# A two-layer attention and expert network on one core: softmax denominators by block transposes with additions a head at a time, query and key projections as half-column pairs, and another order of steps among the experts

## What is computed

```python
def layer(x, attention, network):
    xn = layernorm(x)
    return x + attention(xn) * silu(network(xn))

# first layer: attention over the 16 heads of each token; network of 16 experts, two chosen per token:
routed = combine[:, 15:16] * flat
for e in range(15):
    y = (silu(flat @ gate_w[e]) * (flat @ up_w[e])) @ down_w[e]
    routed = routed + combine[:, e:e+1] * y      # and a shared expert with a convolution in its gate

# second layer: attention over the 1024 tokens of a sequence, 16 heads of 64
xr = xn / norm(xn) * sqrt(128) * (gamma + 1)
q, k, v = split(xr @ w_qkv)
sim = (q * 64 ** -0.5) @ k.T
out = softmax(sim, axis=-1) @ v                  # the denominator is the sum of exp over the keys
s = out.reshape(b, n, 1024) @ w_out
# network: three layers of 512 with weights of -1, 0 and 1 and a scale each
```

## Time and profile before

| | |
|---|---|
| median of 3 runs | 1085.93 us (1085.88 to 1086.94) |
| profiled execution | 1085.6 us, span 1083.8 us |
| PE busy | 1065.5 us (98%) |
| DVE, POOL, ACT busy | 799.9, 794.4, 577.2 us |
| granted clock of PE, mean | 0.999 |

### The profile page before, as it was taken

One profiled execution on the slowest core, in us unless ns is written; L12 is line 12 of the kernel. 1 busy time (PEld: TensorE's weight loads), 2 busy tenths in 40 slices (PEclk: granted clock), 3 DMA queues, 4 the chain that ended last, 5 costly groups with the idle time before them and its releaser, 6 DMA issues.

```text
span 1083.8 us, 21982 instructions
## 1 busy us (share of the span) xinstructions
PE 1065.5 (98%) x8715; PEld 675.5 (62%) x8715; DVE 799.9 (74%) x1249; ACT 577.2 (53%) x923; POOL 794.4 (73%) x515
## 2 busy tenths in 40 slices
PE   9999999899999999999999999999999999999998
PEld 7898898777655455455455555555555455467886
DVE  4658866587776878877887887887888877895553
ACT  4634453565555555555555555555555555654442
POOL 5778997645567898898898899899899898940000
PEclk9999999999999999999999999999999999999999
DMA  7323234533100000200000000000000000000000
GB/s 234 134 80 100 101 117 127 159 112 107 35 1 1 1 1 2 108 1 1 1 1 1 1 2 1 1 2 1 1 2 2 1 1 2 1 1 10 11 1 20
DMA packets 32678, 40.22 MB, mean 37 GB/s; under 512 B 4544, under 2 KB 24384, under 8 KB 31296
## 3 DMA queue, kind: packets, MB, share of 16 engines
q1 hardware_dynamic: 32256, 38.80, 10.9%
q10 hardware_dynamic: 320, 0.01, 0.0%
HBM read 28.97 MB, written 9.70 MB: 36 GB/s over the span
## 4 chain that ended last, share of the span: by engine, by line
PE 74%; DVE 3%; ACT 1%; issue 1%; SPq 0%; DMA 0%; DVEq 0%; ACTq 0%
PE o_ps L1735 21%; PE mx_ps L1688 7%; PE st_ps L1707 5%; PE st_ps L1713 5%; PE st_ps L1710 5%; PE bank L2142 3%; PE bank L2143 3%; PE bank L2144 3%; PE mx_ps L1626 3%; PE pj_ps L1640 3%; PE pj_ps L1632 2%; PE mx_ps L1620 2%; PE st_ps L1719 1%; PE mx_ps L1622 1%; PE mx_ps L1621 1%; DVE mx_part L1947 1%
## 5 line engine op out<-in xcount | busy, mean ns | idle before, releaser
L2054 POOL TENSOR_TENSOR acc<-acc,prob 128x1024 f32<-128x1024 f32 x192 | 468.7, 2441 | 47.3 <-ACT prob L1881 37.1
L1881 ACT ACTIVATE prob<-st_ps 128x1024 f32<-128x1024 f32 x256 | 248.6, 1023 | 197.7 <-PE st_ps L1719 103.6
L1735 PE MATMUL o_ps<-prob,v_cur 128*64 128x512 f32 x1024 | 246.4, 602 | 0.0
L1944 DVE TENSOR_REDUCE mx_part<-mx_ps 128x1 f32<-128x512 f32 x258 | 164.7, 666 | 58.3 <-PE mx_ps L1688 58.3
L1947 DVE TENSOR_REDUCE mx_part<-mx_ps 128x2 f32<-128x1024 f32 x78 | 93.5, 1199 | 60.8 <-PE mx_ps L1688 60.8
L1735 PEld LDWEIGHTS o_ps<-prob,v_cur 128*64 128x64 f32 x1024 | 63.8, 136 | 108.9 <-issue 72.7
L1969 DVE RECIPROCAL rden<-rden 128x128 f32<-128x128 f32 x128 | 119.5, 934 | 0.0
L1688 PEld LDWEIGHTS mx_ps<-k_hi,q_hi 64*128 64x128 f32 x414 | 46.5, 183 | 107.4 <-issue 72.6
L1688 PE MATMUL mx_ps<-k_hi,q_hi 64*128 64x512 f32 x414 | 111.8, 457 | 1.4 <-DVE mx_part L1947 0.6
L2054 POOL TENSOR_TENSOR acc<-prob 128x1024 f32<-128x1024 f32 x32 | 76.6, 2393 | 34.1 <-ACT prob L1881 33.0
L1713 PE MATMUL st_ps<-q_hi,d_lo 64*128 64x512 f32 x512 | 100.9, 390 | 0.0
(11 more groups left out here) (404 smaller groups left out, 2209.7 us busy)
## 6 DMA issues: line engine op xcount, KB each, us to landing
w_tile<-w_rows SPq DMA_DIRECT2D x72, 128.0 KB, 2.9
v_rows<-ha_v SPq DMA_DIRECT2D x8, 1024.0 KB, 4.2
ha_vt<-v_rows SPq DMA_DIRECT2D x16, 512.0 KB, 4.1
q_max<-mx_turned SPq DMA_DIRECT2D x128, 1.0 KB
h_w<-in_h SPq DMA_DIRECT2D x2, 1024.0 KB, 7.9
w_raw<-in_w SPq DMA_DIRECT2D x8, 192.0 KB, 3.7
head_wkv<-in_wkv SPq DMA_DIRECT2D x2, 512.0 KB, 4.8
m_w<-in_m SPq DMA_DIRECT2D x3, 256.0 KB, 3.0
```

Of the source, the lines that this page charges most:

```text
L1735: mm = pe.matmul(o_ps[rows(h), :], v_cur[:, m % 2, j, rows(h)], prob[:, (16 * m + slot) % RING, h, :], start=(j == 0), stop=(j == KT - 1), ...
L1881: act.activation(prob[:, n % RING, :, :], st_ps[:, slot % 2, :, :], ACT.Exp, scale=SCALE).then_inc(s_exp, 1)
L1944: dve.reduce_max(mx_part[:, h, i, keys:keys + 1], maxima_banks(q, n)[h], AX_X).then_inc(s_mxr, 1)
L2054: pool.tensor_tensor(total, old, new, ALU.add).then_inc(s_acc, 1)
```

## The change

It has five parts.

- **Denominators.** POOL adds a head at a time, 28 additions of 512 columns instead of 14 of 1024. DVE turns `acc` of a half (1024 columns) in blocks of 32 x 32 (`turned`) and sums each run of 32, so that `den_part` holds one sum a token for 32 partitions. PE adds the four blocks of partitions by `lanes`, with 16 columns a head instead of 512. ACT copies 16 columns, DVE inverts them, and a second block transpose of their repetition spreads them out into `rden`. `INVERT` goes; `DEN_TURN`, `DEN_SUM`, `DEN_BACK` and `NORMALIZE` say in which batch each step stands. The `den` unit of half 1 moves from batch 1 to batch 2 on PE.
- **Queries and keys.** A `qk` unit is two plain `F32` products of 64 columns of weights each, for the two heads, instead of three `F32R` ones of 128. The splits of `w_raw` and of `xr` go, on ACT, DVE and POOL.
- **Experts.** On ACT, `gate` and `sq` stand ahead of the Silu of the iteration.
- **Handover.** `e.scalar_x` is a turn earlier on ACT; on PE the gates of iteration 3 and the down product of iteration 0 stand between the last turns of the first attention.
- **End of the attention.** The low parts of the last network's weights `h2` are made on POOL behind its additions, no longer on DVE; x's split for chunk 0 moves from DVE to ACT and POOL; the last units stand in other places (`AFTER_END`).

```diff
-    FIRST = ("sq",)
+    FIRST = ("gate", "sq")
...
     def scalar(act, n):
         k, e = n // EPAIRS, n % EPAIRS
-        if n < ALL:
-            act.wait_ge(s_g, n + 1)
-            act.activation(g_ps[n % 2], g_ps[n % 2], ACT.Silu).then_inc(s_sg, 1)
         kn, names = norms(n)
         for name in names:
             if name in FIRST:
                 scalar_norm(act, kn, name)
+        if n < ALL:
+            act.wait_ge(s_g, n + 1)
+            act.activation(g_ps[n % 2], g_ps[n % 2], ACT.Silu).then_inc(s_sg, 1)
...
+    DEN_TURN, DEN_SUM, DEN_BACK = {1: (1, -1), 4: (0, 0)}, {2: (1, -1), 5: (0, 0)}, {3: (1, -1), 6: (0, 0)}
+    NORMALIZE = {5: (1, -1), 7: (0, 0)}
...
-    AFTER = {1: ("den", 1), 3: ("out", 0), 5: ("den", 0), 7: ("out", 1)}
+    AFTER = {2: ("den", 1), 3: ("out", 0), 5: ("den", 0), 7: ("out", 1)}
+    AFTER_END = {1: ("out", 0), 2: ("den", 1), 7: ("out", 1)}
...
-            hi, lo = xr_hi[:, chunk(q, half), :], xr_lo[:, chunk(q, half), :]
-            pe.matmul(to, w_hi[:, p, tile(t)], hi, start=True, stop=False)
-            pe.matmul(to, w_hi[:, p, tile(t)], lo, start=False, stop=False)
-            mm = pe.matmul(to, w_lo[:, p, tile(t)], hi, start=False, stop=True)
+            for h in range(2):
+                of = slice(t * P + h * HD, t * P + h * HD + HD)
+                mm = pe.matmul(to[rows(h), :], w_raw[:, p, of], xr[:, chunk(q, half), :], start=True, stop=True,
+                               skip_group_check=True)
...
-            pe.wait_ge(s_acc, ADDS * q + 7 * (half + 1))
+            pe.wait_ge(s_turns, den_done(q, u[1], "summed"))
             for h in range(2):
-                mm = pe.matmul(pj_ps[rows(h), :], c.ones[:, 0:HD], acc[:, half, h, :],
+                mm = pe.matmul(pj_ps[rows(h), 0:DEN], lanes[:, :], den_part[:, h * DEN:h * DEN + DEN],
                                start=True, stop=True, skip_group_check=True)
...
-            act.activation(rden[:, half, :], pj_ps[:, :], ACT.Copy).then_inc(s_den, 1)
+            act.activation(den_out[:, :], pj_ps[:, 0:DEN], ACT.Copy).then_inc(s_den, 1)
...
-        dve.reciprocal(part, part).then_inc(s_rcp, 1)
+    def vector_den_turn(dve, q, half):
...
+        dve.wait_ge(s_acc, 2 * (ADDS * q + 7 * (half + 1)))
+        dve.transpose(turned[:, :], acc[:, half, :, :].rearrange("p h n -> p (h n)")).then_inc(s_turns, 1)
+
+    def vector_den_sum(dve, q, half):
+        dve.wait_ge(s_turns, den_done(q, half, "turned"))
...
+        dve.reduce_sum(den_part[:, :], turned[:, :].rearrange("p (n r) -> p n r", r=LANES), AX_X).then_inc(s_turns, 1)
+
+    def vector_den_back(dve, q, half):
+        dve.wait_ge(s_den, 2 * q + half + 1)
...
+        dve.reciprocal(den_rcp[:, :], den_out[:, :]).then_inc(s_turns, 1)
+        dve.wait_ge(s_turns, den_done(q, half, "inverse"))
+        dve.transpose(rden[:, half, :].rearrange("p (n r) -> p n r", r=LANES),
+                      den_rcp[:, :].unsqueeze(2).to_broadcast([P, DEN, LANES])).then_inc(s_turns, 1)
...
-        pool.tensor_tensor(total, old, new, ALU.add).then_inc(s_acc, 1)
+        for h in range(2):
+            new, total = prob[:, (16 * m + slot) % RING, h, :], acc[:, half, h, :]
+            old = prob[:, (16 * m + slot - 1) % RING, h, :] if j == 1 else total
+            if j > 1:
+                pool.wait_ge(s_acc, 2 * (ADDS * m + 7 * half + j - 2) + h + 1)
+            pool.tensor_tensor(total, old, new, ALU.add).then_inc(s_acc, 1)
...
                 head.tensor_outs(pe, TURNS - 2, 1)
+                e.tensor_gates(pe, 3)
                 head.tensor_y(pe, TURNS - 2)
                 head.tensor_outs(pe, TURNS - 1, 0)
                 head.tensor_outs(pe, TURNS - 1, 1)
+                e.tensor_down(pe, 3)
                 head.tensor_y(pe, TURNS - 1)
```

More of the change, by code:

```diff
@@ L1111, in sync_load @@
               .then_inc(s_wload[i % 2], 16)
-    def parts(n):
-        return n // EPAIRS - 2 if n % EPAIRS == 0 and n >= 2 * EPAIRS else None
     def gates(kn):
@@ L1394, in second_attention @@
     mx_row, mx_turned = early.sb("mx_row", [P, BLOCK], F32R), early.sb("mx_turned", [P, BLOCK])
-    w_hi, w_lo = (pairs.sb(n, [P, PAIRS, W_QK], F32R) for n in ("w_hi", "w_lo"))
+    LANES, DEN = 32, CH // 32
+    turned = early.sb("turned", [P, 2 * CH])
+    lanes, den_part, den_rcp = (early.sb(n, [P, size]) for n, size in (("lanes", HD), ("den_part", 2 * DEN), ("den_rcp", DEN)))
+    den_out = early.sb("den_out", [P, DEN])
     q_raw = e.res[:, :]
@@ L1466, in after @@
     def after(m, b):
-        if b not in AFTER:
-            return None
-        q = m + AHEAD[AFTER[b]]
-        return (q, AFTER[b]) if 0 <= q < STEPS else None
+        places = AFTER if m < STEPS else AFTER_END
+        if b not in places:
+            return None
+        q = m + AHEAD[places[b]]
+        return (q, places[b]) if 0 <= q < STEPS else None
     def maximum(m, b, second):
@@ L1998, in vector @@
         was = (m, b - 1) if b else (m - 1, BATCHES - 1)
-        if after(*was) and AFTER[was[1]][0] == "out":
+        if after(*was) and after(*was)[1][0] == "out":
             vector_add_out(dve, *after(*was))
@@ L2040, in gpsimd @@
             gpsimd_cut(pool, m + 1)
-        if (m, slot) == XR_LO_AT:
-            e.gpsimd_xr_lo(pool, LAST)
         if j == 0:
             return
-        new, total = prob[:, (16 * m + slot) % RING, :, :], acc[:, half, :, :]
-        if j == 1:
-            old = prob[:, (16 * m + slot - 1) % RING, :, :]
-            if m:
-                pool.wait_ge(s_pj, count_of[m - 1, ("den", half)])
-        else:
-            old = total
-            pool.wait_ge(s_acc, ADDS * m + 7 * half + j - 1)
-        pool.wait_ge(s_exp, 16 * m + slot + 1)
-        pool.tensor_tensor(total, old, new, ALU.add).then_inc(s_acc, 1)
+        if j == 1 and m:
+            pool.wait_ge(s_turns, den_done(m - 1, half, "turned"))
+        pool.wait_ge(s_exp, 16 * m + slot + 1)
+        for h in range(2):
+            new, total = prob[:, (16 * m + slot) % RING, h, :], acc[:, half, h, :]
[3 more added lines that the diff above has]
+            pool.tensor_tensor(total, old, new, ALU.add).then_inc(s_acc, 1)
     s.BATCHES = BATCHES
@@ L2165, in split @@
     def split(pe, w):
[L2167 to L2170 removed]
+        pe.wait_ge(s_lo_w, cut_by[w])
     def tensor_first(pe, k, m):
@@ L2401, in two_layers @@
         late = Region(nc, FIRST)
-        e = experts(nc, c, first, head, x, xn, xr, xr_hi, xr_lo, eps, weights_t, moe_w, w_rows, w_tiles, at, only, keep)
-        t2 = second_attention(nc, c, head, e, a, xr, xr_hi, xr_lo, early, pairs, late, at)
+        e = experts(nc, c, first, head, x, xn, xr, eps, weights_t, moe_w, w_rows, w_tiles, at, only, keep)
+        t2 = second_attention(nc, c, head, e, a, xr, early, pairs, late, at)
         behind = Region(nc, late.at)
@@ L2540, in _ @@
                             end.scalar_split(act, i)
+                        if m == END and b == SPLIT_END:
+                            end.scalar_x(act)
                 end.scalar_table(act, ACT.Silu)
@@ L2628, in _ @@
                         t2.gpsimd(pool, m, slot)
+                        if m == END and slot == 2 * SPLIT_END + 2:
+                            end.gpsimd_x(pool)
                         if m < END and slot % 2:
@@ L2631, in _ @@
                                 end.gpsimd_split(pool, i)
-                for i in range(end.TILES - HT, end.TILES):
+                for i in range(end.EARLY, end.TILES):
                     end.gpsimd_split(pool, i)
```

191 lines of the change are left out of this document (84 added, 107 removed).

## The result

The changed kernel takes 1076.11 us (median of 4, 1074.19 to 1079.9) against 1085.98 (median of 4, 1085.88 to 1086.94): a ratio of 0.9913, 95% interval 0.9898 to 0.9927. It is faster by 9.9 us, where I forecast 26.1, and it lies outside my range of 1052 to 1074. No rival of mine describes what happened, and the number near rival (c), 1074, is a coincidence: the steps came out as forecast.

A forecast was written before the change was run, and what follows sets the result against it. PE was taken to bound the kernel, busy 41.00 of 41.00 us in attention steps. Terms -21.1 - 1.8 + 0.7 + 2.0 - 3.3 - 2.0 - 0.6 = -26.1 us gave a median of 1059.8 us, range 1052 to 1074.

The forecast's parts named there:

- rival (c): Attention steps: POOL takes over at 1.375 us a half, a step 40.1 instead of 39.7 us; 1074 us, 10%.
- the four units ahead: Query and key units ahead of the attention loop on PE: each pays its own change of form, +0.7 us for all.
- The tail: End of attention: h2's low parts go to POOL, PE's waits at the last denominator and 962.21 go; -0.6 us.
- my two signs of being wrong: Attention steps: forecast is wrong if POOL never waits, or if PE's busy share falls below 97%.
- Denominators on PE: Attention on PE: a denominator unit falls from 0.86 to 0.20 us, -0.66 each, times 32, -21.1 us.
- Queries and keys: Attention steps on PE: a float32 pair replaces three products, -0.03 us a unit times 60, -1.8 us.
- Case (e): Query and key units on PE: by the skill's four passes, 60 units 0.23 us dearer; 1075 us, 2%.
- DVE's stall at batch 2: Attention steps: PE waits 0.15 us a step for DVE's q_lo, in 14 steps +2.0 us (0 to +5).
- rivals (a) and (b): Attention, DVE's long transposes: at 2.5 ns a column 1097 us, 5%; at 1.6 ns a column 1071 us, 10%.
- Experts: Among the experts: gate and square ahead of the Silu shorten PE's waits, 3.9 us in all, by 3.3 us.
- Handover: First attention to experts: earlier x_hi, gates 3 and down 0 fill PE's waits; -2.0 of 2.3 us.
- Case (d): Among the experts: the new orders only move the stalls, as the waiting Silu holds h; 1065 us, 8%.

The follow-up runs named there:

- run 1: Changed kernel, but in the last step POOL waits, before its third slot's additions of half 1, until DVE has made the normalisation o_n; 1059.59 us.

## Why the prediction was wrong

Three starts of PE cut the run into stretches: the first product with `q_max` of the attention's first step and of the last half step, and the end. The second of them, before and after:

```profile
936.35 0.51 PE L1719 MATMUL st_ps<-q_max,minus 64*128 64x512 f32 x2
```

```profile
910.38 0.50 PE L1703 MATMUL st_ps<-q_max,minus 64*128 64x512 f32 x2
```

The first stands at 302.17 before and at 297.80 after. So the experts and the handover gave 4.4 us, the stretch of the steps went from 634.2 to 612.6 (-21.6), and what is left went from 147.4 to 163.8 (+16.4): together -9.6, the difference of the spans. With the pause of run 1 the three are -4.8, -21.4 and +0.1, together -26.1, which is my sum. My terms for them were -4.6 (experts, handover, the four units ahead), -20.9 and -0.6; that they meet to a tenth is luck. The tail's -0.6 doesn't come even there: PE waits 0.7 us for `den_part` and 1.2 for `act03lo` and `act02lo` instead.

**The step that failed** is in two places of the prediction. In the paragraph on POOL: "Halves wait only for the one before last, so that wait goes." I booked this as a gain of POOL and did not ask who used that wait. And the tail: "-0.6 us", with DVE's four low parts of `h2` put on POOL "behind its last add", as if work there cost nobody anything. Measured with the change it is +16.4, of which 15.5 is one wait for one DVE instruction and 2.3 the slower clock behind it, less about 1.4 of smaller things. In place of my reasoning the runs show this: in the steps, o_n comes into rows that a wait for ScalarE or an earlier o_n has broken a few instructions before; in the last step POOL is behind, finds every exponential ready, and its row grows from 891, where DVE last got in, to 939.9 through the additions, `x_lo` and the weights' low parts. PE has no queries and keys of a next step to make there and goes through the first half in 17.1 us (893.28 to 910.38), 2.14 a slot, where the first half of the step before took 20.7 (853.72 to 874.45) and POOL needs 2.49 a slot. By the row's end, the work I had moved behind the last addition made the hold 6.6 us longer (933.3 to 939.9); no run leaves out that move alone.

Neither of my two signs of being wrong showed this: POOL waits for ACT in the steps, and PE is busy 39.41 of 39.55 us there. I had given none for the end.

The trace of before had shown the price of such meetings: six additions took 16.34 us at the end. There each side got in once per instruction. I took this for the whole of it, as rival (c) does, which costs the meeting at one instruction more each time.

**What held.**
- Bound: PE 39.41 of 39.55 us in a step, at a clock of 1.00.
- Denominators on PE: a step became 1.4 us shorter. Batch 5 has a `v` unit ahead of the denominator in both kernels, before and after:

```profile
536.45 1.89 PE L1735 MATMUL o_ps<-prob,v_cur 128*64 128x512 f32 x8
...
539.12 0.50 PE L1688 MATMUL mx_ps<-k_hi,q_hi 64*128 64x512 f32 x2
```

```profile
564.41 1.89 PE L1719 MATMUL o_ps<-prob,v_cur 128*64 128x512 f32 x8
566.12 0.24 PE L1616 MATMUL pj_ps<-den_part,lanes 128*64 128x16 f32 x4
566.30 0.50 PE L1672 MATMUL mx_ps<-k_hi,q_hi 64*128 64x512 f32 x2
```

  From start to start it is 2.67 us before and 1.89 after: -0.78 a denominator for my -0.66. Behind a unit of 64-column products and without a denominator it is 1.82 us (544.50 to 546.32), so the small product costs 0.07 where I had 0.20, and less than my lower end of 0.13.
- Queries and keys: -0.04 at batch 0 (from the maxima's start to the next batch 541.56 - 538.51 = 3.05 us, before 3.09), nothing at batch 3 (2.98 us to the output product in both), for my -0.03 a unit. The four ahead of the loop cost nothing that shows, for my +0.7. The Trainium skill (FP8 and Floating Point Precision, TensorE Precision Notes) has true FP32 in four passes, and by that rule the units would have been 0.23 dearer by my estimate. Case (e), which takes it so, did not come.
- DVE's stall at batch 2: PE idles 0.14 us a step for it, for my 0.15 (0.20 by the starts: 551.43 - 551.05 = 0.38 us from the small product to the next batch, 0.18 in batch 5).
- DVE's new pieces, as rows of the changed kernel show them, against my 1.25, 1.20 and 0.71:

```profile
L1952 DVE STREAM_TRANSPOSE turned<-acc 128x1024 f32<-128x1024 f32 x30 | 37.0, 1234 | 0.0
L1959 DVE TENSOR_REDUCE den_part<-turned 128x32 f32<-128x1024 f32 x30 | 36.1, 1203 | 0.0
L1967 DVE STREAM_TRANSPOSE rden<-den_rcp 128x512 f32<-128x512 f32 x30 | 21.3, 712 | 1.0
```

  So rivals (a) and (b) are out: (1234 - 712) / 512 = 1.02 ns a column.
- POOL: 14.94 us for twelve halves, 2.49 a slot, for my 2.5; it still waits for ScalarE in each step, so (c) did not come. Its busy time in a step is 37.47 us for my 36.6, and 38.73 for 37.9 with a weight's low part.
- DVE's busy time did not drop to 32.2 us a step: it is 33.55, though its new pieces took what I gave. The runs don't single out where the rest comes from.
- Experts: -2.6 (-2.4 by the medians) for -3.3: the waits for x fell only from 2.4 to 1.8; the squares' 1.5 went whole. Handover: -1.8 for -2.0. Case (d), stalls that only move, did not come.

## What the runs showed of the hardware

- **DVE can be shut out by a long row of POOL.** An instruction of DVE with two SBUF operands got in at the end of POOL's instruction under way where POOL's row was up to 9 instructions long, and not before the row's end where it was 13 or longer (the list above; 22.82 us at most). A gap of 0.03 us was enough to start a new row. All that were held were this one o_n, 128x512 in float32, beside `TENSOR_TENSOR` instructions of POOL, nearly all of 512 columns; no run has other forms in a long row. The Trainium skill (SBUF — State Buffer, section "SBUF: two separate sides") has the two engines share a port pair under an exclusive lock; against an instruction of DVE with two SBUF inputs it holds when POOL's reads SBUF, and whichever starts first keeps it "for the whole instruction". The short rows agree: DVE's 0.68 us become at most 1.7, one instruction more. The long rows don't: in the changed kernel DVE let 20 ends of POOL's instructions pass.
- Transposes and reductions with one SBUF operand were not held: `turned` took 1.23 to 1.25 us and `den_part` 1.20 to 1.22 beside POOL's rows, and o_n's neighbours that read PSUM were not held either. A copy did wait for POOL's instruction under way: in the kernel with one pause a cast from SBUF to SBUF took 1.51 us beside POOL and 0.43 once POOL had ended.

```profile
940.84 1.51 DVE L2324 CAST act10hi<-whole 128x512 fp32r<-128x512 f32 x1
...
953.69 0.43 DVE L2324 CAST act21hi<-whole 128x512 fp32r<-128x512 f32 x1 [0.96 <-ACT whole L2262]
```

- Whether the number of instructions or the time since the last gap sets the point near 11 stays open. At 11, where both occur, 14.5 us had passed since DVE last got in where it got in again and 15.2 where it was held. In the changed kernel POOL's instructions overlap more as the row grows (1.27 us long at a row's start and 1.29 to 1.33 further on, at the same 1.24 from start to start), but the overlap doesn't decide. In the kernel with o_n in batch 0, o_n was held at 668.94 with an overlap of 0.04 us (an addition of 1.28 us begun at 667.78, the next at 669.02), and in the changed kernel it got in at 889.96 with 0.05 to 0.06.
- In the 15.5 us without a product TensorE's granted clock was 0.60 on the mean, and 0.54 in the 5 us behind them, so mostly at 1.2 GHz; that cost 2.3 us.
